# A causal attention layer with experts: where the mask of the row maxima's diagonal tiles is added, and a unit loop written out

## The reference

```python
Q, K = apply_rope(split_heads(x @ Wq.T)), apply_rope(split_heads(x @ Wk.T))
logits = einsum('bhnd,bhmd->bhnm', Q, K) * scale
logits = where(tril(ones(seq_len, seq_len)), logits, -inf)
probs = softmax(logits, axis=-1)
attn = einsum('bhnm,bhmd->bhnd', probs, V)
```

## Time and profile before

| | us |
|---|---|
| median of 3 runs (1318.79 to 1322.03) | 1320.54 |
| the profiled execution, its own time | 1329.57 |
| its span, first to last instruction | 1327.7 |

### The profile page before, as it was taken

How to read it: one execution, slowest core, us unless ns; L and a number is a source line. 1 busy time by engine, 2 the same in 40 slices (tenths; PEclk the granted TensorE clock), 3 DMA queues, 4 the chain that set the end, 5 groups by cost and what they waited for, 6 DMA issues and landing times. The chain is left out here.

```text
span 1327.7 us, 19905 instructions
## 1 busy us (share of the span) xinstructions
PE 1106.4 (83%) x5928; PEld 575.0 (43%) x5929; DVE 704.8 (53%) x1404; ACT 480.9 (36%) x722; POOL 265.2 (20%) x366
## 2 busy tenths in 40 slices
PE   8972899998999999999728999999949999999500
PEld 4540234433444344343225666666625555555300
DVE  5992878886888877887024454444221111111154
ACT  2440056664666666666702222222202222222100
POOL 2334022221222222222112111111120000000254
PEclk9995599998999999999968999999969999999855
DMA  7558334553453443440081111110011111111133
GB/s 251 142 142 150 45 54 64 97 93 55 84 94 59 88 88 56 89 91 10 13 254 40 48 48 48 47 47 17 17 44 40 40 40 39 40 39 40 51 119 111
DMA packets 80501, 97.35 MB, mean 73 GB/s; under 512 B 27456, under 2 KB 68160, under 8 KB 77120
## 3 DMA queue, kind: packets, MB, share of 16 engines
q1 hardware_dynamic: 72080, 78.54, 27.8%
q0 software_dynamic: 3456, 9.44, 2.2%
q10 hardware_dynamic: 4912, 8.66, 2.0%
HBM read 64.76 MB, written 31.46 MB: 72 GB/s over the span
## 5 line engine op out<-in xcount | busy, mean ns | idle before, releaser
L591 DVE TENSOR_REDUCE maxima<-max_ps 128x1 f32<-128x512 f32 (+3 forms) x608 | 384.6, 660 | 120.5 <-PE max_ps L447 61.3
L538 ACT ACTIVATE probs<-scores_ps 128x1024 f32<-128x1024 f32 (+3 forms) x384 | 290.5, 809 | 164.5 <-PE scores_ps L467 163.0
L443 PE MATMUL max_ps<-k_stack,q_stack 96*128 96x512 bf16 (+3 forms) x768 | 249.1, 347 | 43.4 <-DMA q_stack<-q_parts 32.5
L467 PE MATMUL scores_ps<-q_stack,k_stack 99*128 99x512 bf16 (+3 forms) x768 | 183.7, 328 | 6.1 <-issue 4.0
L443 PEld LDWEIGHTS max_ps<-k_stack,q_stack 96*128 96x128 bf16 x768 | 75.0, 98 | 233.9 <-DVE maxima L591 173.0
L487 PE MATMUL out_ps<-probs,v_ones 128*32 128x512 f32 (+3 forms) x1536 | 164.5, 500 | 3.9 <-POOL probs L675 1.8
L675 POOL TENSOR_SCALAR_AFFINE_SELECT probs<-probs 128x512 f32<-128x512 f32 x128 | 81.2, 634 | 380.5 <-ACT probs L538 380.5
L1420 DVE TENSOR_TENSOR hidden_e<-silu_e,up_ps_e 128x512 f32<-128x512 f32 x40 | 27.5, 688 | 191.2 <-PE up_ps_e L1297 191.2
L447 PE MATMUL max_ps<-mask,ident_bf 128*128 128x128 bf16 x512 | 105.1, 230 | 0.0
L1297 PE MATMUL gate_ps_e<-gate_sb,rows_t 128*128 x160 | 80.9, 629 | 21.3 <-ACT rows_t L1342 21.0
L1489 POOL DMA_INDIRECT fetched<-expert_results,fetch_i x32 | 32.4, 1011 | 298.4 <-DMA expert_results<-result 276.5
(11 more groups left out here) (147 smaller groups left out, 1141.5 us busy)
## 6 DMA issues: line engine op xcount, KB each, us to landing
k_stack<-k_parts SPq DMA_DIRECT2D x96, 128.0 KB, 4.3
q_stack<-q_parts SPq DMA_DIRECT2D x96, 128.0 KB, 7.5
q_parts<-parts SPq DMA_DIRECT2D x32, 192.0 KB, 3.2
k_parts<-parts SPq DMA_DIRECT2D x32, 192.0 KB, 3.0
rows_in<-expert_rows SPq DMA_DIRECT2D x40, 128.0 KB, 2.0
expert_results<-result SPq DMA_DIRECT2D x40, 128.0 KB, 1.7
x_t<-in_x_cols SPq DMA_DIRECT2D x8, 512.0 KB, 11.2
heads_rows<-heads_out SPq DMA_DIRECT2D x32, 128.0 KB, 3.4
```

What stands on the lines that cost most here:

```text
L443: last = nc.tensor.matmul(bank, q_stack[:ROWS, u.slot, h0 + k, t * P:(t + 1) * P], k_stack[:ROWS, u.slot, h0 + k, chunk * BLOCK:chunk * BL ...
L467: last = nc.tensor.matmul(scores_ps[:, pair, k, n0:], k_stack[:ROWS_MAX, u.slot, h, mt * P:(mt + 1) * P], q_stack[:ROWS_MAX, u.slot, h, c ...
L538: nc.scalar.activation(probs[:, s % RING, 2 * pair:2 * pair + 2, n0:], scores_ps[:, pair, :, n0:], ACT.Exp).then_inc(exp_done, 1)
L591: nc.vector.tensor_reduce(maxima[:, u.slot, chunk, h0:h0 + heads, t], max_ps[:, n % 2, :heads * keys].rearrange("p (h k) -> p h k", h=head ...
```

## The change

In the 16 diagonal pieces of a single head, PE leaves the mask's matmul out. DVE takes the mask in instead: in place of `tensor_reduce` a `tensor_tensor_reduce` adds `mask_wide` (f32, 512 wide, 0 but for the last 128 columns, so that its tail fits pieces of 384 and of 512) and takes the maximum of the sums. It must also write the sums; they go as bf16 to `masked_out`, of six buffers in turn, and nobody reads them. A `stand` ahead of it carries the wait for the piece and one for the piece four before, which frees the buffer. The diagonal pieces of 2 and 4 heads (0, 1, 2, 15, 20, 21) keep the mask on PE. POOL makes `mask_wide` with a memset and a select ahead of the memset of `v_ones`, and DVE's first piece waits for it. `each_unit` writes all 16 units out on every engine.

```diff
-def each_unit(eng, step):
-
-    for i in range(2):
-        step(Unit.number(i))
-    with eng.Fori(0, (UNITS - 4) // Unit.RING) as turn:
-        for k in range(2, 2 + Unit.RING):
-            step(Unit(turn * Unit.RING + k, k % Unit.RING, turn + k // Unit.RING))
-    for i in range(UNITS - 2, UNITS):
+def each_unit(step):
+
+    for i in range(UNITS):
         step(Unit.number(i))
...
+        mask_wide = b.sb("mask_wide", [P, BLOCK])
+        masked_out = b.sb("masked_out", [P, 6, BLOCK], BF16)
...
@@ find_max on PE
-                        diagonal = chunk == t // BT
+                        diagonal = chunk == t // BT and heads > 1
...
@@ reduce on DVE
                     dve.wait_ge(piece_done, PIECES * u.i + n + 1)
+                    if chunk == t // BT and heads == 1:
+                        wait(dve, piece_reduced, PIECES * u.i + n - 3)
+                        stand(dve, dve_stood)
+                        nc.vector.tensor_tensor_reduce(
+                            masked_out[:, n % 6, :keys], max_ps[:, n % 2, :keys], mask_wide[:, BLOCK - keys:], 1.0,
+                            NEG, ALU.add, ALU.max, maxima[:, u.slot, chunk, h0:h0 + 1, t]).then_inc(piece_reduced, 1)
+                        continue
                     nc.vector.tensor_reduce(maxima[:, u.slot, chunk, h0:h0 + heads, t],
...
+            dve.wait_ge(wide_made, 1)
             reduce(Unit.number(0), range(PIECES))
...
+            nc.gpsimd.memset(mask_wide[:], 0.0).then_inc(consts_half, 1)
+            pool.wait_ge(consts_half, 2)
+            tail = mask_wide[:, BLOCK - P:]
+            nc.gpsimd.affine_select(out=tail, in_=tail, compare_op=ALU.is_ge, fill=NEG, base=0,
+                                    pattern=[[-1, P]], channel_multiplier=1).then_inc(wide_made, 1)
             nc.gpsimd.memset(v_ones[:], 1.0).then_inc(consts_made, 1)
```

More of the change, by code:

```diff
@@ L382, in attend @@
         heads_stored = [b.sem("heads_stored0"), b.sem("heads_stored1")]
-        pool_stood = b.sem("pool_stood")
+        pool_stood, dve_stood, wide_made = b.sem("pool_stood"), b.sem("dve_stood_a"), b.sem("wide_made")
         block = ctx.enter_context(nc.Block())
@@ L422, in _ @@
             send_neg(Unit.number(0))
-            each_unit(sp, step)
+            each_unit(step)
             store_heads(Unit.number(UNITS - 1), 1)
@@ L526, in _ @@
             pe.wait_ge(k_ones, 1)
-            each_unit(pe, step)
+            each_unit(step)
             times_v(Unit.number(UNITS - 1), STEPS - 1)
@@ L555, in load_weights @@
             def load_weights(u):
-                if isinstance(u.i, int) or u.slot == 1:
+                if not 2 <= u.i < UNITS - 2 or u.slot == 1:
                     return
@@ L577, in _ @@
             negate(Unit.number(0))
-            each_unit(act, step)
+            each_unit(step)
             copy_out(Unit.number(UNITS - 1), 1)
@@ L629, in _ @@
             reduce(Unit.number(1), range(EARLY))
-            each_unit(dve, step)
+            each_unit(step)
             normalise(Unit.number(UNITS - 1), 1)
@@ L689, in _ @@
             split_neg(Unit.number(0))
-            each_unit(pool, step)
+            each_unit(step)
 def by_batch(eng, step):
```

## The result

| | before | changed |
|---|---|---|
| runs, median | 1320.54 us | **1326.25 us** |
| runs, lowest to highest | 1318.77 to 1322.18 (7) | 1324.45 to 1328.29 (7) |
| ratio | | 1.0037, 95% interval 1.0022 to 1.0053 |
| profiled execution, own time / span | 1329.57 / 1327.7 us | 1327.33 / 1325.5 us |
| mean granted clock | 0.914 | 0.915 |

The change makes the kernel slower by 0.4%: more than a measurement of it is uncertain, 5 us above the forecast of 1321 and inside the range of 1311 to 1342. The two profiled executions say the opposite, 2.2 us faster. That contradiction is the first thing to be explained.

A forecast was written before the change was run, and what follows sets the result against it. Inside a unit of 31.30 us PE's own work was put at 29.0, the rest waits, nearly all for DVE. Loop -6.6, units +5.6 and prologue +0.9 summed to -0.1 us: 1329.5 profiled, 1321 us median, range 1311 to 1342.

The forecast's parts named there:

- rival 4: Writing out does not remove the stall: code read first time waits elsewhere, or the 4.05 us are the profiler's; 1328, chance 0.08.
- rival 1: On DVE, the read-out waits for the main instruction's end, 0.165 us more a piece; 1332 us, chance 0.24.
- The loop, -6.6: Writing units out removes the first jump's longer stretch: 4.05 us of PE waiting, the rest slow clock; -6.6 us in all.
- The mask on PE: 16 matmuls of 0.06 us a unit, 0.96 us, leave PE; gained only where PE sets the pace.
- pieces 3 to 6: In a unit, PE sets the pace there and gains 0.06 us at each, but then waits for ACT's or DVE's work.
- The read-out, 0.075 a piece: The new DVE instruction's accumulator read-out adds 0.075 us for each piece, bounds 0 and 0.32; the main instruction costs nothing more.
- Rivals 1 and 2: DVE's read-out waits for the main instruction's end, 1332 us (0.24); a far dearer instruction, 0.3 a piece, 1356 us (0.10).
- The stand, 0.11 where DVE waits: The stand ahead of DVE's new instruction costs 0.11 us where DVE waits for the piece, nothing where it is there already.
- The unit: Pieces 34 to 37 +0.28, 3 to 10 +0.10, 26 to 29 0: +0.38 us a unit, +5.6 over 14.7 units.
- the prologue: PE has only pieces there, at clock 0.5; 12 rounds of two changed pieces at 0.08 us each, +0.9 us.
- Signs to look for: 256 mask rows, DVE's new pieces 0.675 us apart, idle about 0.15 behind PE's end, units 31.7, no stretch of 37.9.
- Rival 3: On DVE, the stand is hidden or the main instruction a little shorter; only the loop's gain is left: 1314 us, chance 0.16.

## Why the prediction was off, point by point

The measured 1326.25 lies in the range of 1311 to 1342 and 5 us above the forecast. Of the rivals that the range takes in, only the second half of rival 4 is near to what moved the number; rival 1, which had three times its chance, gave a slower kernel for a reason that the runs refute. That the number came so near is in part luck, as the terms of the unit show.

- **The loop, -6.6: this is the step that failed.** The step read the profile rightly (1329.57 to 1322.1 on writing out) and then took "the same difference off at the end", as if the median carried the stall too. It doesn't, by the runs' times: the 9.0 us between profile and median were mostly the stall itself. So 6.6 us of gain were credited to a median that had nothing to gain. The second half of rival 4, "the 4.05 us are the profiler's", which gave 1328 and got a chance of 0.08, is nearest to what the runs showed, though "the profiler's" is more than is known. The step also put the loop's register instructions at nothing. In the trace of before the unit ahead of the loop takes 31.24 and those in it up to 31.31, and written out all take 31.24: they cost up to 0.07 a unit, under 1 us, which the runs can't tell.
- **The mask on PE: mis-sized.** Taken as 0.06 on each of two paths, 0.12, and at 26 to 29 as all eaten by the stands. It gives 0.53 a unit (31.24 to 30.71), from the stretches where PE sets the pace. The sentence that failed is the one on pieces 3 to 6, that PE "gains 0.06 at each, but then waits": the 0.18 gained by piece 6 was kept, and at 27 to 29 another 0.23 came, of which the stands take 0.14 and not all.
- **The read-out, 0.075 a piece: mis-sized.** With the main instruction it costs 0.06 to 0.07 in a whole unit: the next main one starts 0.60 to 0.62 after the one before, and the maximum is there 0.70 after the start, where the plain reduction ends at 0.69. Rivals 1 and 2, which needed over 0.10 and 0.3 a piece, fell; the read-out does not wait for the main one's end (0.62 after its start, 0.69 long). The rule of the Trainium skill's page "VectorE: DVE Perf Modes", section "The DRAIN you can't avoid", which was rival 1, does not hold this pair; its section "Two Vector instructions with no wait between them" had it right.
- **The stand, 0.11 where DVE waits: mis-sized twice.** It costs up to 0.18 there (0.22 behind PE's end, not 0.04), and there are four such places in a unit's path, not two, since DVE waits at pieces where the timeline prints no idle time. 0.72 in place of 0.22. The price of the near row, 0.11, is just what the stand costs ahead of the plain reduction; ahead of the new instruction, with two waits, it is 0.07 more. Of the error of 0.50 the two places left out are 0.36, the price at the other two 0.14.
- **The unit.** Predicted +0.38 (31.7), from -0.12 for masks, +0.28 for read-outs and +0.22 for stands. Measured: -0.53, +0.07 and +0.72, which is +0.26 (31.50 - 31.24). Three wrong terms whose errors, -0.41, -0.21 and +0.50, nearly cancel: that the sum looks better than its parts is luck. For the whole stage +6.5 was taken and the runs give 1326.25 - 1321.57 = +4.7. (Of it the prologue was put at +0.9; its last piece ends 1.4 later than in the written-out kernel, counted from the first.) Add the 6.6 that were not there to gain: 1321 + 6.6 - 1.8 = 1325.8, and 1326.25 was measured.
- **Signs to look for.** 256 masks gone, units alike (but for 31.81), no stretch of 37.9: as written. Distance of pieces 0.60 where DVE sets the pace and 0.65 to 0.71 from 8 to 10, where 0.675 was written; idle behind PE's end 0.22 where 0.15 was; units of 31.5 where 31.7 was. Rival 3 (1314, "the stand is hidden") is what the kernels without the stand's wait do, 1313 to 1314 us, but by other terms.

The change on the whole: its idea is good for 0.6%, and the place of one wait takes it back. Had the loop stayed, it would have cost another 18.6 us (1344.9 against 1326.25).

## What to carry to other kernels

When an instruction can't carry two waits, put the one that ends last on the instruction itself and the one that is long met on the extra one in front: 12.4 us here (1326.25 to 1313.8), for two lines in another order. Before a stall in a profile is counted as a gain, see whether the runs' median has it; if the profiled execution lies above all the runs by about the stall, it probably doesn't. And look at the jumps again after adding instructions to a loop: 48 more in the body that do nothing, 16 a unit, cost 23 us here.

## What the runs showed of the hardware

- A wait on an instruction of its own ahead of a VectorE operation starts that operation 0.15 us (one wait, plain reduction) or 0.22 us (two waits, the new instruction) behind the releasing matmul's end, a wait on the operation 0.04. The Trainium skill, page "Perfetto Trace Analysis", section "Per-instruction lifecycle: what the profiler-reported window actually captures", describes why: an engine's instruction is passed to a queue that waits while the sequencer goes on, but a sequencer's own instruction holds the sequencer until its wait is over, and only then is the next one read. The runs agree (the stand with its wait met costs nothing).
- VectorE's add-and-maximum with accumulator, two f32 sources of which one is in PSUM, bf16 written, takes as long for 512 columns as the plain reduction (0.69), and its read-out of 0.08 adds at most 0.02 to a distance of 0.60.
- The jump back of a VectorE loop stalled it for 5.4 to 5.9 us each time with bodies of 308 and 356 instructions, and not with one of 260; the loop's start lay elsewhere in each. PE, with 699 matmuls in its body, stalled 4.05 us at the first of three jumps in both profiled executions of before, and by the runs' times hardly ever otherwise.
